# Cross attention of a decoder layer in fixed slots: the work of one batch pair spread over its neighbours

## The reference

```
q = (layernorm(x) @ Wq)            # 16 heads of 128
k, v = ctx @ Wk, ctx @ Wv          # ctx: 8 x 64 x 128; 8 heads of 128, each used by two query heads
scores = q . k / sqrt(128)         # 256 x 64 for each batch and head, masked
x = x + (softmax(scores) @ v) @ Wo
```

## Time and profile before

| | |
|---|---|
| median of 3 runs | 1014.76 us (1014.35 to 1014.99) |
| the profiled execution | 1014.01 us |
| span of its trace | 1012.3 us |
| mean granted clock of TensorE | 0.944 |
| busy: PE, DVE, ACT, POOL | 86%, 55%, 43%, 26% |
| first and last instruction of the cross attention | about 453.7 and 717.4 us |

### The profile page before, as it was taken

One profiled execution on the slowest core, in us unless ns is written; L12 is line 12 of the kernel. 1 busy time (PEld: TensorE's weight loads), 2 busy tenths in 40 slices (PEclk: granted clock), 3 DMA queues, 4 the chain that ended last, 5 costly groups with the idle time before them and its releaser, 6 DMA issues. The chain is left out here.

```text
span 1012.3 us, 15924 instructions
## 1 busy us (share of the span) xinstructions
PE 871.9 (86%) x5190; PEld 737.4 (73%) x5191; DVE 561.3 (55%) x1591; ACT 434.5 (43%) x1102; POOL 260.6 (26%) x450
## 2 busy tenths in 40 slices
PE   5999999999999999977969797887633999999990
PEld 4788889888988889866566574846412788888870
DVE  5777666665666565644847568464676233232235
ACT  3666656655665656633424134331260222222220
POOL 1333233322233223320111101111211344444430
PEclk9999999999999999998989899898775999999995
DMA  8002000000000000002520606034590111111117
GB/s 290 1 2 97 1 2 1 2 1 1 2 1 21 2 1 1 2 7 98 119 48 15 151 0 149 16 71 97 203 375 20 38 52 52 52 52 52 47 41 254
DMA packets 45575, 61.61 MB, mean 61 GB/s; under 512 B 3472, under 2 KB 36368, under 8 KB 45392
## 3 DMA queue, kind: packets, MB, share of 16 engines
q1 hardware_dynamic: 39664, 48.58, 16.7%
q0 software_dynamic: 3744, 10.23, 3.2%
q10 hardware_dynamic: 2112, 2.10, 0.6%
HBM read 34.81 MB, written 9.31 MB: 44 GB/s over the span
## 5 line engine op out<-in xcount | busy, mean ns | idle before, releaser
L302 POOL TENSOR_TENSOR prob<-prob,rinv 128x128 f32<-128x128 f32 (+1 forms) x256 | 124.2, 506 | 306.9 <-DVE rinv L394 304.7
L365 DVE TENSOR_TENSOR pT_lo<-bank_t,pT_hi 128x384 fp32r<-128x384 f32 x128 | 70.5, 551 | 97.8 <-ACT pT_hi L317 97.8
L328 ACT ACTIVATE prob<-masked,negmax 128x128 f32<-128x128 f32 (+1 forms) x256 | 113.9, 454 | 0.0
L317 ACT ACTIVATE pT_hi<-bank_t 128x384 fp32r<-128x384 f32 x128 | 62.7, 490 | 114.2 <-PE bank_t L507 114.2
L1519 DVE TENSOR_TENSOR f_xT_lo<-bank_o,f_xT_hi 128x256 fp32r<-128x256 f32 x39 | 16.6, 425 | 128.1 <-ACT f_xT_hi L1366 128.1
L427 DVE CUSTOM_DVE_ANT_0 masked<-bank_s,causal 128x128 f32<-128x128 f32 (+1 forms) x256 | 80.2, 351 | 9.2 <-PE bank_s L40 9.2
L38 PE MATMUL bank_s<-kT_hi,qT_hi 128*128 128x128 f32 (+1 forms) x256 | 80.9, 316 | 0.0
L38 PE MATMUL bank_y<-WprojT_hi,oT_hi 128*128 128x256 f32 x256 | 72.0, 281 | 3.2 <-DVE oT_lo L365 3.2
L1664 PE MATMUL bank_y<-f_Wo,f_interT 128*128 x312 | 73.9, 380 | 0.8 <-ACT f_interT L1361 0.8
L40 PE MATMUL bank_y<-WprojT_hi,oT_lo 128*128 128x256 f32 x256 | 71.6, 280 | 0.0
L39 PE MATMUL bank_y<-WprojT_lo,oT_hi 128*128 128x256 f32 x256 | 71.4, 279 | 0.0
(11 more groups left out here) (305 smaller groups left out, 2436.1 us busy)
## 6 DMA issues: line engine op xcount, KB each, us to landing
b_VW_hi<-b_VWs_hi SPq DMA_DIRECT2D x32, 256.0 KB, 4.8
b_VW_lo<-b_VWs_lo SPq DMA_DIRECT2D x32, 256.0 KB, 5.0
f_W_lo<-in_L_ffn_w_kernel_dram SPq DMA_DIRECT2D x16, 512.0 KB, 9.6
f_Wo<-in_L_ffn_wo_kernel_dram SPq DMA_DIRECT2D x8, 512.0 KB, 9.3
stage<-n_L_attn_weight_qkv_dram SPq DMA_DIRECT2D x5, 512.0 KB, 6.9
WqT<-in_L_xattn_Wq_dram SPq DMA_DIRECT2D x1, 2048.0 KB, 7.5
b_wo<-in_L_xattn_Wo_dram SPq DMA_DIRECT2D x1, 2048.0 KB, 9.2
xn_rows<-f_xn SPq DMA_DIRECT2D x4, 512.0 KB, 9.5
```

Of the source, the lines that this page charges most:

```text
L302: pool.tensor_tensor(prob[:, u % 3, a:b], prob[:, u % 3, a:b], rinv[:, u % 4, i:i + 1].to_broadcast([P, b - a]), ALU.mult)\
L317: act.activation(dst.hi, src, ACT.Copy).then_inc(half[n], 1)
L328: act.activation(prob[:, u % 3, a:b], masked[:, u % 2, a:b], ACT.Exp, scale=-1.0, bias=negmax[:, u % 4, i:i + 1], accum_out=rowsum[:, u % ...
L365: dve.tensor_tensor(dst.lo, src, dst.hi.bitcast(F32), ALU.subtract).then_inc(free[n], 1)
```

## The change

The loop and the lists are replaced by straight code for 18 slots. Slot (p, t) holds the scores of tile t of pair p, the output of the tile two slots earlier, the transposes of the tile one slot earlier, and some of the products of the next pair: k in slot 0, v in slot 1, vw in slot 2, xt and m in slot 3. Two more slots at the end finish the last two tiles. `start` makes all products of pair 0, vw too, ahead of the first slot. The order on each engine follows from the code, `Order` only counts the uses of the banks. The 16 transfers of 256 KB of a pair become 8 of 512 KB, four for each batch: those of batch b of pair p are issued when all vw of the pair are copied and the outputs of batch b of the pair before are made. ACT and DVE wait for all transfers of a pair before they write VWs again.

```diff
-        front = [(("xt", c), ("q", "t")[c], "both") for c in range(HC)]
-        front += [(("k", i), ("q", "t")[i], "act") for i in range(2)]
...
-        body = (s_step(0) + vw_step((0, 1)) + s_step(1) + nxt[2:4] + quiet("next_ln", 0) + quiet("sum", 0)
-                + vw_step((2, 3)) + quiet("move", 0) + vw_step((4, 5)) + quiet("sum", 1) + vw_step((6, 7))
-                + quiet("move", 1) + nxt[4:6] + quiet("next_xn", 0) + t_step(0) + s_step(2) + t_step(1) + s_step(3)
-                + quiet("sum", 2) + y_step(0) + y_step(1) + nxt[0:2] + quiet("sum", 3)
-                + t_step(2) + nxt[6:8] + y_step(2) + nxt[8:11] + t_step(3) + nxt[11:] + y_step(3))
...
+        start = [("k", 0, 0), ("k", 0, 1), ("v", 0, 0), ("v", 0, 1)] + [("m", 0, i) for i in range(NH // 4 * HC)] + \
+                [("xt", 0, c) for c in range(HC)] + [("vw", 0, g) for g in range(NG)]
...
+            return [(name[0], p + 1) + name[1:] for name in {
+                (0, 0): [("k", 0)], (0, 1): [("k", 1)], (1, 0): [("v", 0)], (1, 1): [("v", 1)],
+                (2, 0): [("vw", g) for g in range(3)], (2, 1): [("vw", g) for g in range(3, NG)],
+                (3, 0): [("xt", c) for c in range(HC)] + [("m", i) for i in range(3)],
+                (3, 1): [("m", i) for i in range(3, NH // 4 * HC)]}[t, part]]
...
+        SLOTS = [(p, t) for p in range(PAIRS) for t in range(TT)] + [(PAIRS, 0), (PAIRS, 1)]
+        ROT = {0: ("y1",), 1: ("y1",), 2: ("s0", "s1", "y1"), 3: ("q", "t", "y1")}
...
+        for i, name in enumerate(start):
+            use_fill(name, ("q", "t", "s0", "s1", "o0", "o1", "y1"), i)
...
+                def move(p, b):
                     for src, dst in ((VWs.hi, VW.hi), (VWs.lo, VW.lo)):
+                        for h in range(2):
+                            sp.dma_start(dst[h * S2:(h + 1) * S2, :, b, :].bitcast(F32),
+                                         src[b * S2:(b + 1) * S2, :, h * HID:(h + 1) * HID].bitcast(F32))\
+                                .then_inc(VW_moved[b], 16)
+                for p in range(PAIRS):
+                    for g in range(NG):
+                        at = ("vw", p, g)
+                        sp.wait_ge(free[order.bank(at)], order.free(at))
+                    for b in range(2):
+                        if p > 0:
+                            sp.wait_ge(y_done, TT * (p - 1) + 2 * b + 2)
+                        move(p, b)
...
+                def high(name):
...
+                    if name[0] == "vw" and name[1] > 0 and name[2] == 0:
+                        for moved in VW_moved:
+                            act.wait_ge(moved, 64 * name[1])
...
             @block.vector
...
+                for p, t in SLOTS:
+                    if p < PAIRS:
+                        softmax_shift(p, t)
+                    if earlier(p, t, 2):
+                        residual(*earlier(p, t, 2))
+                    if p < PAIRS:
+                        if t < 3:
+                            softmax_sum(p, t)
+                        for name in fills_at(p, t, 0):
+                            low(name)
+                        if t == 3:
+                            softmax_sum(p, t)
...
+                        if t == 0:
+                            layer_norm_stats(p + 1)
+                        if t == 1:
+                            mean_and_variance(p + 1)
+                            normalize(p + 1)
...
             @block.tensor
...
+                for p, t in SLOTS:
+                    if p < PAIRS:
+                        scores(p, t)
+                    if earlier(p, t, 2):
+                        outputs(*earlier(p, t, 2))
+                    if p < PAIRS:
+                        for name in fills_at(p, t, 0):
+                            fill(name)
+                    if t < 3 and earlier(p, t, 1):
+                        transposes(*earlier(p, t, 1))
+                    if p < PAIRS:
+                        for name in fills_at(p, t, 1):
+                            fill(name)
+                    if t == 3:
+                        transposes(*earlier(p, t, 1))
```

More of the change, by code:

```diff
@@ L579 @@
 class Order:
[L585 to L628, removed]
@@ L630, in before, with __init__, use, bank @@
-    def before(self, p, name):
-        return self._of(p, name)[2]
+    def __init__(self):
+        self.at, self.last, self.counts = {}, {}, {}
+    def use(self, bank, name, who):
+        full, half, free = self.counts.get(bank, (0, 0, 0))
+        self.counts[bank] = (full + 1, half + (who == "both"), free + (who in ("both", "act")))
+        self.at[name] = (bank, who, self.counts[bank], self.last.get(bank))
+        self.last[bank] = name
+    def bank(self, name):
+        return self.at[name][0]
@@ L635, in cross_attention, with who, full, half @@
+    def who(self, name):
+        return self.at[name][1]
+    def full(self, name):
+        return self.at[name][2][0]
+    def half(self, name):
+        return self.at[name][2][1]
+    def free(self, name):
+        return self.at[name][2][2]
+    def before(self, name):
+        return self.at[name][3]
 def cross_attention(nc, cm, ctx_in, mask, Wq, Wk, Wv, Wo):
@@ L702, in cross_attention @@
         prob_ready = sem("prob_ready")
[L703 removed]
+        VW_moved = [sem("VW_moved0"), sem("VW_moved1")]
+        y_done = full["y0"]
         y_added = sem("y_added")
[L706 to L710 removed]
@@ L712, in s_step @@
[L712 to L727, removed]
@@ L811, in run @@
                             .then_inc(prob_ready, 1)
[L813 removed]
+                        if t == 1 and p + 1 < PAIRS:
+                            power(p + 1)
             @block.scalar
             def _(act):
[L817 to L824 removed]
@@ L841, in _ @@
-                passes(act, run)
+                def high(name):
+                    n, who = order.bank(name), order.who(name)
+                    dst, src = dst_of(name)
+                    if name[0] == "vw" and name[1] > 0 and name[2] == 0:
+                        for moved in VW_moved:
+                            act.wait_ge(moved, 64 * name[1])
+                    act.wait_ge(full[n], order.full(name))
+                    act.activation(dst.hi if who == "both" else dst, src, ACT.Copy)\
+                        .then_inc(half[n] if who == "both" else free[n], 1)
@@ L843, in _, with low @@
             @block.vector
             def _(dve):
-                def copy_out(p, name):
-                    who = order.who(p, name)
-                    n = order.bank(p, name)
-                    if who == "both":
+                def low(name):
+                    n = order.bank(name)
+                    if order.who(name) == "both":
                         dst, src = dst_of(name)
-                        dve.wait_ge(half[n], order.half(p, name))
+                        if name[0] == "vw" and name[1] > 0 and name[2] == 0:
+                            for moved in VW_moved:
+                                dve.wait_ge(moved, 64 * name[1])
+                        dve.wait_ge(half[n], order.half(name))
```

368 lines of the change are left out of this document (170 added, 198 removed).

## The result

The changed kernel takes 974.98 us (median of 4 runs, 974.84 to 977.30), the kernel before 1014.82 beside it: ratio 0.9614, 95% interval 0.9597 to 0.9630, so some 39 us faster. The forecast was 974 with a range of 964 to 988. The profiled execution took 974.84 us, its span 973.1.

A forecast was written before the change was run, and what follows sets the result against it. PE bounds the kernel, idling about 10 us a pair, mostly for VW transfers. Start 477.5 + pair 0 50.0 + 2 x 52.0 + last pair 41.2 + low clock about 4 = 676.7, 40.7 saved: 974 us, range 964 to 988.

The forecast's parts named there:

- 4 us that had been added apart for low stretches: Two low-clock stretches, behind the 2.9 us pause in slot (0,0) and in the tail, about 2 us each.
- The start: Everything up to the first scores, forecast to end at 477.5, with k and v at 5.6 us, mostly at low clock.
- Slots 0 and 1: Slots with the next pair's k and v products: 8.4 us each in pair 0, 9.4 each in full slots.
- Slot 2: Slot with the next pair's vw products: 14.4 us of PE work plus 1.2 of waits, 15.6.
- half of the bytes are 10.6: Transfers into VW: sixteen took 21.1 us, so half the bytes were taken to need 10.6.
- the overwrite of VWs costed at nothing: Slot 2: last transfers land 8.2 into it, ACT wants to copy at 7.7, DVE busy until 8.8; no cost.
- the first rival: Slot 1's transfers need 13 us and land late: 2.4 us in pairs 1 and 2, 979; chance 0.10.
- Slot 3: Slot with the next pair's xt and m: 15.6 us of PE work plus waits of 1.2 and 0.7, 17.6.
- The last pair: Four slots of 7.5 us, 30.1, plus a tail of 11.1 with uncovered copies: 41.2 together.
- The rival that waits for banks bring it down inside the pairs: Bank waits ending slots 2 and 3 of three pairs lower the clock: 10 to 13 us more, 984 to 987; chance 0.08.
- the granted clock falls inside the pairs: Sign named beforehand that would show the forecast wrong; the stretch's mean clock was to rise to 0.97 or more.
- 24.2 us of waits: PE's four waits for transfers into VW before each pair's first output in the kernel before; forecast to go.

The follow-up runs named there:

- e3: Changed kernel with a second bank for the second k and second v product sets (s1 in slot 0, t in slot 1): 973.94 us, ratio 0.9600.
- e9: Changed kernel with each 512 KB transfer cut into two of 256 KB, same bytes and places of issue: 975.89 us, ratio 0.9622.
- e11: Changed kernel with separate semaphores for hi and lo transfers, and DVE's row sums ahead of its lo copies in slot 3: 973.99 us, ratio 0.9614.
- e10: Changed kernel with DVE's softmax row sums ahead of its lo copies in slot 3: 974.29 us, ratio 0.9615.
- e1: Changed kernel with only four of eight groups of VWs moved for pairs 1 to 3: 969.7 us, ratio 0.9573.
- e7: Kernel before, same 16 transfers of 256 KB, those of batch 0 ahead of batch 1 in each half: 1017.67 us, ratio 1.0039.
- e4: Changed kernel with the transposes of slot 2 ahead of all eight vw products, on every engine: 976.80 us, ratio 0.9621.
- e8: Changed kernel with batch 0 transfers of pairs 1 to 3 held back to batch 1's place, slot 1 of their own pair: 1013.64 us, ratio 0.9990.
- e5: Kernel before with only two of every four groups moved, VW set to zero once at the start: 986.29 us, ratio 0.9717.
- e2: Changed kernel with separate semaphores for hi and lo transfers, ACT waiting for hi only, DVE for lo only: 972.75 us, ratio 0.9606.
- e12: Changed kernel with separate hi and lo semaphores, second banks for k and v, and row sums ahead of copies in slot 3: 969.63 us, ratio 0.9585.

## Why the prediction was right, and where it was off

The forecast came out within 1 us, and that closeness is in part luck: the three full pairs took 7.8 us longer than their slots were summed to, against which stood a start that came 2.1 sooner and 4 us that had been added apart for low stretches. Point by point, with the end of the cross attention forecast at 676.7 and measured at 679.25:

- **The start** was forecast at 477.5 and came at 475.37. The step that was mis-sized is the 5.6 us for k and v, "mostly at the low clock". They took 3.67, at a clock of 1.00, behind a pause of the expected 2.8 us. From there to the first scores are 20.23 us, where the forecast has 22.1. In e3, e9 and e11 the same code took 21.6, in e10 23.07, so the forecast lies among the outcomes that occur.
- **Slots 0 and 1** were right to 0.1 us where the forecast has a full slot (9.4). The second of pair 0 took 9.82 because the low clock behind the pause of 2.46 us falls into it; that loss, 1.5 against e1, was forecast apart as 2.
- **Slot 2** is the step that failed in its mechanism: "half of the bytes are 10.6", and the overwrite of VWs costed at nothing. Without the late landing the slot takes 15.23 (e1), near the 15.6 forecast. With it, 17.61 and 19.07. It is the first rival, which had been given a chance of 0.10, at its numbers: 13.06 us from issue, 10.6 into the slot, and in pair 1 2.0 us over the forecast. In pair 2 it came with a low stretch, 1.5 more, which that rival did not have. The text said beforehand that ACT or DVE waiting for a transfer would show the step wrong, and ACT waits 3.2 and 3.4 us.
- **The halving** went wrong in two ways. One is a part that doesn't shrink with the bytes. In pair 0 the kernel after moves 4 MB in 24.0 us (from 475.32 to the landing of the last, issued at 488.14, 11.2 us later), and later 2 MB in 13.0; so 11.0 go with each 2 MB and 2.0 stay. With the 256 KB transfers of e9 it is 11.1 and 1.3. By itself this adds 0.7 to 1.0 us to a half. The other way is larger: these transfers move more slowly than those of the kernel before. The 4 MB of pair 0 took 21.1 us there, 21.7 grouped by batch in fours (e7), 23.5 in e9 and 24.0 in the change. Grouping in fours is thus worth 0.5 us here (1.0 on the mean of the pairs) and the size of 512 KB 0.5. The 1.8 between e7 and e9 no run takes apart: in e9 eight in a row read the same 64 partitions, and two in a row write the same ones. Its cause stays open. The Trainium skill ("DMA: Bandwidth & Descriptors", Anatomy of one DMA) also has a fixed part, of about 2.0 us, and by its rate the 2 MB would have landed in an estimated 6.8 us. That section is on transfers that GpSimd issues, and these are issued by SP; for them the measured 13.06 decides.
- **Slot 3** was forecast at 17.6 and took 17.87. PE's two waits there are 0.69 and 0.74 for lo copies of M, 1.4 together, where 1.9 was forecast, and the rest of the slot is 0.8 longer than its sum of distances.
- **The last pair** took 42.05 against 41.2: the first of the two last transposes left PE waiting 2.40 us instead of 1.84, which is 0.7 in the distance from transposes to output (3.44 where the second has 2.71). The forecast low stretch in the tail did not come in this execution; in e3, e4, e8, e9 and e10 it did.
- **The clock.** The rival that waits for banks bring it down inside the pairs came true at one place, against the six that it counted: behind the wait of 1.90 us inside slot 2 of pair 2, worth about 1.3. By the text's own sign (the granted clock falls inside the pairs) the forecast was wrong there. In pair 1 PE waits 1.73, 0.56, 0.69 and 0.74 us and the clock is 1.00. So an oscillation such as the Trainium skill describes ("TensorE: Matmul & The Clock Gate", A second HAM failure mode: psum-queue depth-cycling) did not show in this rotation; the clock fell behind single pauses of 1.90 and 2.46 us.
- **What the gain is made of.** The text names 24.2 us of waits first, and e5 agrees: without the transfers' waits and the clock behind them the kernel before is 33.5 us shorter. The order by slots adds 11.8 when the bytes are halved on both sides (e5 and e1), and the change's own late transfers and low stretches take 7.6 back; together 37.7 from the first scores on. What stays open is why the same start runs at one clock in one execution and at another in the next.

Beyond the working: the feed-forward part ended 1.0 us sooner than "as a whole", so in the profiled execution the errors are -2.1 at the start, +1.8, +2.3 and +3.8 in the first three pairs, +0.9 in the last, -4 for the two low stretches that had been added apart, and -1.0 behind: +1.6 in all, where the medians differ by 1.0.

## What to carry to other kernels

A transfer that is moved off the path has two ends: ask when its destination is wanted, and when its source may be written again; here the second was late by 2 us after the first had been cured of 24. Don't halve a measured landing time along with its bytes: a part of it is fixed, and transfers that are cut and ordered otherwise may move at another rate. And a slack elsewhere may be what hides a transfer: of 5.6 us shaved off two earlier slots 4.2 were given back, and taking apart the signals of the high and low parts won back 2.0.

## What the runs showed of the hardware

- Moves between places of SBUF ran at 160 to 205 GB/s, counted from the first issue to the last landing: sixteen of 256 KB, 4 MB, in 20.5 to 21.1 us (before), 21.5 to 21.8 grouped in fours by batch (e7) and 23.5 in eights (pair 0 of e9), eight of 512 KB in 23.7 to 25.1 (pair 0 of the kernel after and of e3, all pairs of e8), four of 512 KB in 13.06 and 13.24.
- The same pause does not always bring the clock down. Behind 2.82 us at the start it stayed at 1.00 in the kernel after, e1, e2, e4 and e12, was 0.66 on the mean of 5 us in e3, e9 and e11, and about 0.50 in e8 and e10. Behind 2.46 us in slot (0,0) it fell in the kernel after, e4, e8, e9, e10 and e11 and stayed in e1 and e2. In slot 2 there is no loss behind pauses of 0.97 to 1.85 us and one of 2.05 (pair 2 of e3, 17.97 us), and a loss of 1.3 to 1.5 us behind 1.90 (pair 2 of the kernel after), 1.98 (pair 0 of e3, pair 2 of e4) and 1.99 (pair 2 of e10).
- Executions of one kernel differ by 2.5 to 7.6 us in the changed kernel and its variants (974.84 to 977.30 in the kernel after, 972.22 to 979.78 in e4) with the same code, and the slower ones have the lower mean clock: 0.964 and 0.956 in those two of e4. In the traces, one for each kernel, the start, the tail and slot 2 of pair 2 are seen to take part in it.
